# A four-layer graph kernel: the first product with the counts taken into the table stage, and the cells of all edge tiles kept

## What is computed

```python
h = relu(layernorm(x))
# layer 0: three rounds, deg = number of edges that end in a node, dinv = deg ** -0.5 (0 where deg is 0)
y = h; acc = h
for _ in range(3):
    y = segment_sum(y[src] * (dinv[src] * dinv[dst])[:, None], dst)
    acc = acc + y
x = x + acc / 4
# layer 1: one weighted sum over the edges, then two 64x64 matrices
# layer 2: two weighted sums over the edges (Chebyshev, K = 3), a sigmoid and a tanh
# layer 3: attention over the edges with 4 heads, exp of clipped scores
```

## Time and profile before

| | |
|---|---|
| median of 3 runs | 2742.87 us (2740.8 to 2744.53) |
| the profiled execution | 2741.29 us, of which its span is 2739.6 us |
| table stage | to 1558.6 us of the span |
| six products | 1558.6 to about 2161 us |
| attention | to the end |
| busy in the whole span | PE 44%, VectorE 67%, ScalarE 29%, GpSimd 46% |

### The profile page before, as it was taken

How to read it: one execution, slowest core, us unless ns; L and a number is a source line. 1 busy time by engine, 2 the same in 40 slices (tenths; PEclk the granted TensorE clock), 3 DMA queues, 4 the chain that set the end, 5 groups by cost and what they waited for, 6 DMA issues and landing times. The chain is left out here.

```text
span 2739.6 us, 40317 instructions
## 1 busy us (share of the span) xinstructions
PE 1204.0 (44%) x12203; PEld 596.2 (22%) x12203; DVE 1842.0 (67%) x3710; ACT 783.7 (29%) x1927; POOL 1266.8 (46%) x973
## 2 busy tenths in 40 slices
PE   1111111111111111111110169978799629998898
PEld 1111111111111111111110023333343413333334
DVE  9988788888888888888885101111201539999997
ACT  0000000133332223121111300000000229999996
POOL 2788888888888888888888000000000000100001
PEclk6555555555555555555555589999899859999997
DMA  6776776689888889775666998889579282333231
GB/s 222 240 220 191 222 221 182 141 216 222 202 218 217 206 210 221 161 156 125 135 148 130 283 421 355 350 361 416 217 286 366 76 132 84 88 88 88 85 87 48
DMA packets 506207, 550.60 MB, mean 201 GB/s; under 512 B 129536, under 2 KB 452669, under 8 KB 504381
## 3 DMA queue, kind: packets, MB, share of 16 engines
q1 hardware_dynamic: 137773, 303.52, 30.9%
q10 hardware_dynamic: 255792, 245.78, 27.9%
q0 software_dynamic: 112608, 0.85, 9.7%
HBM read 381.75 MB, written 168.31 MB: 201 GB/s over the span
## 5 line engine op out<-in xcount | busy, mean ns | idle before, releaser
L610 POOL DMA_INDIRECT table<-amount,cell x782 | 1210.6, 1548 | 295.8 <-issue 281.1
L431 DVE SCALAR_TENSOR_TENSOR equal<-key_row,keys,masks 128x1280 bf16<-128x1280 f32 (+9 forms) x790 | 692.2, 943 | 0.2 <-DVE parts L417 0.2
L563 PE MATMUL totals<-parts_g,equal 128*128 128x6 bf16 x4345 | 129.0, 167 | 1022.8 <-DVE is_tile L440 1022.6
L283 ACT ACTIVATE w_tile<-cells 128x128 f32<-128x128 f32 x600 | 179.2, 301 | 779.4 <-issue 769.3
L563 PEld LDWEIGHTS totals<-parts_g,equal 128*128 128x128 bf16 x4345 | 122.2, 104 | 1034.3 <-DVE is_tile L440 1034.0
L944 PE MATMUL banks<-tiles,xs_pair 128*64 128x512 f32 (+1 forms) x1512 | 316.5, 567 | 5.8 <-DMA tiles<-counts_dram 5.0
L1257 POOL MEMSET o_t<- 128x64 f32 x1 | 0.2, 151 | 650.6 <-POOLq L719 650.6
L1267 POOL COPY v_tile<-v_all 128x128 f32 x175 | 51.6, 296 | 506.1 <-PE banks_d L1320 432.8
L423 DVE SCALAR_TENSOR_TENSOR equal_tail<-key_row,keys,masks 128x1280 bf16<-128x1280 f32 x156 | 235.2, 1546 | 20.1 <-issue 17.1
L1305 PE MATMUL banks_d<-q,k 96*128 (+2 forms) x700 | 194.5, 368 | 80.3 <-DMA k<-parts_dram 47.1
L1152 ACT ACTIVATE att<-banks_d,shift 128x1024 f32<-128x1024 f32 (+1 forms) x175 | 199.2, 1138 | 76.4 <-PE banks_d L1305 76.0
(11 more groups left out here) (226 smaller groups left out, 1513.0 us busy)
## 6 DMA issues: line engine op xcount, KB each, us to landing
table<-zeros ACTq DMA_DIRECT2D x100, 800.0 KB
cells<-table ACTq DMA_DIRECT2D x24, 3200.0 KB
key_row<-keys_dram SPq DMA_DIRECT2D x79, 640.0 KB
tiles<-counts_dram SPq DMA_DIRECT2D x27, 1664.0 KB, 10.0
tiles<-weights_dram SPq DMA_DIRECT2D x27, 1664.0 KB, 9.5
tiles<-counts_dram SPq DMA_DIRECT2D x27, 1536.0 KB, 8.7
tiles<-weights_dram SPq DMA_DIRECT2D x27, 1536.0 KB, 8.3
weights_dram<-w_tile ACTq DMA_DIRECT2D x24, 1600.0 KB
```

Of the source, the lines that this page charges most:

```text
L283: ins = nc.scalar.activation(w_tile[:, b, s], cells[:, s, :, 0], ACT.Copy, accum_out=deg_parts[:, s, bass.ds(t, 1)])
L431: ins = nc.vector.scalar_tensor_tensor(equal[b][:, OWN_AT[j]:OWN_AT[j + 1]], key_row[:, b, j * P:GE], keys[:, bass.ds(g * G + j, 1)], own_ ...
L563: nc.tensor.matmul(sums, equal[b][:, at:at + P], parts_g[:, b, j, :], start=False, stop=True, skip_group_check=True)
L610: nc.gpsimd.indirect_dma_start(out=table, out_offset=bass.IndirectOffsetOnAxis(ap=cell[:, b, j:j + 1], axis=0), in_=amount[:, b, j, :], in ...
```

## The change

**The first product moves into the table stage.** NPROP falls from 6 to 5, the matrix loads of the second block start with what was the second product. In the table stage the product is done node by node: for each destination tile t PE multiplies the 25 blocks of 128 x 128 counts of that tile (now the stationary side) with the 25 tiles of the scaled features `xs` and adds them up in one PSUM bank, 25 matmuls of 64 columns. 23 of the tiles are loaded back from `counts_dram` by SP, 1.6 MB each in pieces of 512 bytes, into a ring of 3 buffers; tiles 23 and 24 are taken from `c_tile`. VectorE copies each sum into `tmp`. The layer norm, the degrees and `xs` move ahead of this, and ACT takes the two square roots between tile 20 and tile 21 (`ROOTS_AT`).

**The cells and amounts of all 79 groups are kept.** `cell` and `amount` become 790 columns wide, and VectorE's wait for `groups_landed` goes away. GpSimd's loop over groups is written out. To make room several buffers share memory: the ring lies where `equal`, `key_row` and `is_row` were, so its first load waits for PE's last group.

**The end of the table stage.** Tile 23 is loaded into memory of its own, and the last tile's two halves are loaded by SP instead of ACT, behind the 23 blocks; VectorE copies its counts and SP stores them.

```diff
-NPROP = 6
+NPROP = 5
@@ build_matrices, buffers
-    key_row = sb("key_row", [P, 2, GE], F32, c)
-    equal = [sb(f"equal{b}", [P, OWN_AT[G]], BF16, c) for b in range(2)]
+    matches, late = sb("matches", [P, OWN_AT[G]], F32, c), sb("late", [P, 2 * GE + G * P], F32, c)
+    equal = [matches[:].bitcast(BF16)[:, b * OWN_AT[G]:(b + 1) * OWN_AT[G]] for b in range(2)]
+    key_row = late[:, 0:2 * GE].rearrange("p (b r) -> p b r", b=2)
+    blocks_a = [part[:, at:at + T * P].rearrange("p (s d) -> p s d", d=P)
+                for part, at in ((matches, 0), (matches, T * P), (late, 0))]
+    RING_A = len(blocks_a)
-    cell = sb("cell", [P, 2, G], U32, c)
-    amount = sb("amount", [P, 2, G, 2], F32, c)
+    cell = sb("cell", [P, ECP], U32, c)
+    amount = sb("amount", [P, ECP, 2], F32, c)
@@ sync
+            sp.wait_ge(totals_ready, NG)
+            for t in range(T - 2):
+                if t >= RING_A:
+                    sp.wait_ge(sums_ready, t - RING_A + 1)
+                sp.wait_ge(stored[t % 2], 32 * (t // 2 + 2))
+                sp.dma_start(blocks_a[t % RING_A],
+                             counts_dram.rearrange("(s p) d -> p s d", p=P)[:, :, t * P:(t + 1) * P]
+                             ).then_inc(block_landed[t % RING_A], 16)
+            sp.wait_ge(groups_landed, NG)
+            sp.wait_ge(w_split, T - 2)
+            sp.wait_ge(c_split, T - 2)
+            for f, half in enumerate(halves):
+                sp.dma_start(cells[:, half].rearrange("p s c two -> p s (c two)"), last[:, half]
+                             ).then_inc(half_landed[f], 16)
+            for f, half in enumerate(halves):
+                sp.wait_ge(last_copied, f + 1)
+                sp.dma_start(counts_dram.rearrange("(s p) d -> p s d", p=P)[:, half, (T - 1) * P:T * P], c_tile[:, 0, half]
+                             ).then_inc(last_stored, 16)
@@ scalar
+            ROOTS_AT = PAIRS - 2
+            with act.Fori(0, ROOTS_AT) as i:
+                pair(i)
+            act.wait_ge(deg_ready, 1)
+            nc.scalar.activation(scale[:, DINV], clipped[:, 0], ACT.Sqrt).then_inc(root_ready, 1)
+            act.wait_ge(var_ready, 1)
+            nc.scalar.activation(k["stat"][:, 2], k["stat"][:, 1], ACT.Sqrt).then_inc(std_ready, 1)
+            with act.Fori(ROOTS_AT, PAIRS - 1) as i:
+                pair(i)
@@ vector
-                dve.wait_ge(groups_landed, g - 2)
                 choose_cells(g - 1, 1 - b)
+            def read_sums(t):
+                dve.wait_ge(sums_ready, t + 1)
+                at = t % RING_A * BANK
+                nc.vector.tensor_copy(near[:, t], masks[:, at:at + D]).then_inc(sums_read, 1)
@@ tensor
+            pe.wait_ge(xs_set, 1)
+            for t in range(T):
+                if t >= RING_A:
+                    pe.wait_ge(sums_read, t - RING_A + 1)
+                if t < T - 2:
+                    pe.wait_ge(block_landed[t % RING_A], 16 * (t // RING_A) + 16)
+                    block_t = blocks_a[t % RING_A]
+                else:
+                    block_t = c_tile[:, t % 2]
...
+                for s in range(T):
...
+                    ins = nc.tensor.matmul(masks[:, at:at + D], block_t[:, s], xs[:, s], start=(s == 0),
+                                           stop=(s == T - 1))
+                ins.then_inc(sums_ready, 1)
@@ propagating_layers
-            with pe.Fori(0, 3) as prop:
+            with pe.Fori(0, 2) as prop:
                 product(prop, 1)
                 turn_sums(prop)
```

More of the change, by code:

```diff
@@ L185, in build_matrices @@
     FILLED = CHUNK_TILES - 1
+    halves = (slice(0, PAIRS), slice(PAIRS, T))
+    DINV, DIS, NDIS, INV, ROOT, TWICE = range(6)
+    clipped, scale, xs, near = k["clipped"], k["scale"], k["xs"], k["tmp"]
     LAST_ROWS = WHOLE_TILES - FILLED * P
@@ L297, in split_done, with pair @@
                 act.wait_ge(c_split, t + 1)
-            load(0)
-            split(0, 0, 0)
-            with act.Fori(0, PAIRS - 1) as i:
+            def pair(i):
                 for b in range(2):
@@ L307, in _ @@
                     split(t + 1, 1 - b, i + b)
+            ROOTS_AT = PAIRS - 2
+            load(0)
+            split(0, 0, 0)
+            with act.Fori(0, ROOTS_AT) as i:
[6 more added lines that the diff above has]
+                pair(i)
             split_done(T - 3)
-            load(T - 2)
+            load(T - 2, cells_23)
             store(T - 3, 0)
-            split(T - 2, 1, PAIRS - 1)
+            split(T - 2, 1, PAIRS - 1, cells_23)
             split_done(T - 2)
[L314 to L318, removed]
             store(T - 2, 1)
@@ L326, in _ @@
                 ins.then_inc(w_split, 1)
[L327 to L331, removed]
+                act.wait_ge(w_split, T + f)
+                act.dma_start(weights_dram.rearrange("(s p) d -> p s d", p=P)[:, half, (T - 1) * P:T * P], w_tile[:, 0, half]
+                              ).then_inc(last_stored, 16)
             act.wait_ge(turned_ready, 1)
@@ L639, in _ @@
-            group(1, 1)
-            with pool.Fori(1, NG // 2) as i:
-                for b in range(2):
-                    group(2 * i + b, b)
-            rest = EDGE_TILES - (NG - 1) * G
-            begin(NG - 1)
-            pool.wait_ge(body_landed, 16 * BODY * (NG - 1))
-            pool.sem_inc(group_taken, 1)
-            scatter(0, range(rest), body_landed)
-            previous_landed(NG - 1)
-            pool.wait_ge(body_landed, 16 * (BODY * (NG - 1) + rest))
+                if g:
+                    pool.wait_ge(body_landed, 16 * BODY * g)
@@ L650, in _ @@
+                pool.sem_inc(group_taken, 1)
+                scatter(range(first, first + TAIL), body_landed)
+                if g:
+                    pool.wait_ge(tail_landed, 16 * TAIL * g)
+                    pool.sem_inc(groups_landed, 1)
+                scatter(range(first + TAIL, min(first + BODY, stop)), body_landed)
+                scatter(range(first + BODY, stop), tail_landed)
+            pool.wait_ge(body_landed, 16 * (BODY * (NG - 1) + EDGE_TILES - (NG - 1) * G))
             pool.sem_inc(groups_landed, 1)
@@ L780, in _ @@
             act.wait_ge(deg_ready, 1)
[L781 to L782 removed]
+            nc.scalar.activation(scale[:, DIS], clipped[:, 1], ACT.Sqrt).then_inc(root_ready, 1)
+            with act.Fori(0, 2) as prop:
                 feed(prop)
```

233 lines of the change are left out of this document (125 added, 108 removed).

## The result

The change made the kernel slightly slower: 2755.3 us (median of 5 runs, 2751.75 to 2758.85) beside 2742.7 us before (5 runs), a ratio of 1.0045 with a 95% interval of 1.0032 to 1.0058. That is 12.6 us more; 2730 was predicted, so the time lies in the stated range (2702 to 2757) and on the wrong side of the kernel before.

A forecast was written before the change was run, and what follows sets the result against it. GpSimd's scatters were taken to pace the table stage up to 1511 us, then the DMA engines to limit it. Product -82.1, block loads +60, stage end +4, GpSimd +5 sum to -13 us: 2730 us, range 2702 to 2757.

The forecast's parts named there:

- A product and its price: Second block: one warm product falls away, -82.1 us, while the new first product again takes 113.8 us.
- so PE keeps up: Table stage: 25 matmuls of a block take 5.79 us on PE, about the block's DMA time.
- The first rival of the list: Table stage: PE limits at 1.2 GHz, 10.1 us a block, stage +85 us, total 2751 us; chance 0.13.
- The rule that I had set beside the sum: PE's blocks: short matmul bursts that wait for DMAs fall back to the low clock in each wait, so blocks run slow.
- My argument against the rival: PE behind 1510 us: it would hardly wait, and steady work had kept the clock up at L982.
- +60 us behind 1510 us: Table stage's end: 10.5 block loads remain for DMA engines already 94% busy, at 5.7 us each.
- xs at 1364: Table stage: tile 20's split ends at 1357.4 us, an estimated 7 us more gives xs and the block products' start.
- +5 was predicted: GpSimd in the table stage: scatters landing late cost +5 us, between bounds of 0 and +58 us.
- The rival of late scatters: GpSimd's table stage: 0.5 us a group over 79 groups, +40 instead of +5, total 2765 us; chance 0.16.
- the stage end near 1628 us: Table stage: its end near 1628 us, with DMA share near 1 from about 1364 us, would show the forecast right.
- VectorE's last choice: Table stage: without its wait VectorE needs 15.6 us a group and is through near 1275 us.
- 54 us of room: DMA engines from 1364 to 1510 us: idle time left for block loads, enough for 9.5 blocks.

The follow-up runs named there:

- the run with VectorE ahead: Kernel before the change, with cell and amount kept for all groups, VectorE's groups_landed waits gone, GpSimd's loop written out, six products kept: 2764.43 us, ratio 1.0085.
- sums apart: Changed kernel with each block matmul written to one of eight bank regions instead of added up in one, first product not summed: 2748.17 us.

## Why the prediction was wrong

*A product and its price.* Right: -82.1 us, and the cold product behind it took 113.0 us where I had written 113.8.

*PE.* This step failed: 25 block matmuls "take 5.79 us", "so PE keeps up". They took 10.67 us. I took the price from L982, where the granted clock was 2.4 GHz behind a product, for a place where PE had been mostly idle at 1.2 GHz through the whole stage. The first rival of the list, with 10.1 us a block, pointed the right way. (It is the one that the paragraph on the rule calls the second.) In the run with extra matmuls six blocks were fast, and behind a wait of 4.76 us all were slow. In the changed kernel PE stood at the low speed for 256 us without a wait between blocks until the last. The rule that I had set beside the sum, of the Trainium skill (TensorE: Matmul & The Clock Gate, "HAM oscillation"), has PE fall to the low clock in its waits: the run with extra matmuls agrees with it on the fall, and it alone does not give the 256 us. My argument against the rival ("it would hardly wait at all, and steady work has kept the clock up at L982") took keeping a speed for reaching it. Why steady blocks do not raise the clock stays open; the runs show only that they did not, and that they kept a high one.

*What bounds the stage.* I let the DMA engines limit the blocks (+60 us behind 1510 us) and in the rival too up to 1510. But at 10.67 us PE needs more for a block than its load does (a block whose pieces moved with no load or store beside them took 5.6 to 7.3 us in this trace; I had 5.7). Taking away all loads gave 5.7 us. The DMA term was sized about right and stood off the path.

*When the blocks start.* 1382 us instead of 1364. The step "xs at 1364" took ScalarE's split of tile 20 from the trace of before, though GpSimd's lateness, a term of its own in my sum, moves it. These 18 us decide the sign: with PE at 10.67 us and `xs` at 1364 the stage would be 93.5 - 18 = 75.5 us longer and the time 2742.9 - 82.1 - 0.8 + 75.5 = 2735.5 us, faster by 0.27%. That is a sum, and no run tests it.

*GpSimd.* +5 was predicted, +33.4 came. Some 15 to 16 are from VectorE's lead (the run with VectorE ahead, the run without loads), some 17.5 from the block loads. The rival of late scatters had put its point of decision at 0.25 us a group and its size at 0.5; 33.4 / 79 = 0.42. But it counted them one for one at the stage's end, where by the chain above they reached it only through the roots.

*The end.* I had the stage end near 1628 us, and it ended at 1652. VectorE's last choice came at 1289.4 us, 14 us later than predicted, which did not matter, since VectorE then waited for ScalarE's roots.

*Two sums of the prediction.* With 54 us of room fixed and 20 blocks to place, 5.2 to 6.2 us a block and 0 to 12 us on GpSimd give 2715 to 2747 us, not 2718 to 2741. And the low clock makes the change a loss from (48.6 + 82.1 - 8 - 5) / 12.5 = 9.4 us a block, not 9.2. Neither changes the account above.

So two rivals came true at once, the low clock with 0.13 and late scatters with 0.16, and hid behind each other in part: added up in the prediction's terms they would have given 2751 + 33 - 5 = 2779 us. With the roots earlier and the blocks in another order the same moved product gives 2%, so moving it was not the fault; what followed it in the lists was.

## What to carry to other kernels

Price a TensorE step by a row at the clock that its place will have, not by the fastest row of its shape; a busy PE did not get faster here by being busy. Where an engine's list puts a small step (two roots of 25 columns) behind a large one, look at who waits for it: two activations of 0.2 us were kept waiting for 79 us, and one tile earlier brought 47 us. And when the pace of one engine is a term of the sum, move every date that was read off it.

## What was unexpected in the hardware

- The same 25 f32 matmuls (128 x 128 against 64 columns) ran at 5.58 us and at 10.67 us a block, each for over 100 us without a gap: high when wide matmuls of 512 columns had gone before, low when not. In one run a wait of 0.49 us left the high clock, and in one of 4.76 us it fell; in another it fell in a wait of 19.28 us.
- The granted clock was shown as 1.00 in the changed kernel's profile and 0.50 in others (roots earlier, sums apart) over the same rows with the same durations. The trace that shows 1.00 has no records of the clock up to some 10 us into the second block. The mean of the clock over an execution was 0.96 in three and 0.66 in two of five runs, with spans of 2750.0 us at either. Before reading the clock column, compare the duration of one instruction. The Trainium skill (TensorE: Matmul & The Clock Gate, "Seeing it yourself") warns that such events have been seen to be unreliable on trn2; these runs agree, in that a trace can lack them.
- A second copy of the key rows, 0.65 MB each, made GpSimd's last scatter 51 us later (1575.6 against 1524.4, one run).
